# Layer 2 attention: probabilities of the later key blocks added onto the first block by POOL and DVE, one block summed by PE, values copied by ACT

## The reference, cut to what matters

```
xn = layernorm(x);  q = xn @ Wq.T;  k, v = split(xn @ Wkv.T)
q, k = 4 * l2norm(q), 4 * l2norm(k)
sim  = q @ k.T, masked above the diagonal
attn = softmax(sim);  out = layernorm((attn @ v) @ Wout.T) * g2
x = x + out + silu_gated_ffn(xn)
```

## Time and profile before

| | |
|---|---|
| median of three runs | 1303.96 us |
| the profiled execution's own time, and its span | 1300.34 us, 1298.5 us |
| busy over the span: PE, DVE, ACT, POOL | 1168.2, 892.5, 669.9, 466.3 us |
| weight loads (PEld) | 800.5 us |
| one body of layer 2 (974 to 1054 us) | 80.00 us, of which the rounds take 57.3 |
| DMA over the span | 23 GB/s mean |

### The profile page before, as it was taken

One profiled execution on the slowest core, in us unless ns is written; L12 is line 12 of the kernel. 1 busy time (PEld: TensorE's weight loads), 2 busy tenths in 40 slices (PEclk: granted clock), 3 DMA queues, 4 the chain that ended last, 5 costly groups with the idle time before them and its releaser, 6 DMA issues. The chain is left out here.

```text
span 1298.5 us, 27029 instructions
## 1 busy us (share of the span) xinstructions
PE 1168.2 (90%) x8812; PEld 800.5 (62%) x8812; DVE 892.5 (69%) x2474; ACT 669.9 (52%) x1294; POOL 466.3 (36%) x695
## 2 busy tenths in 40 slices
PE   4999999999999994798199899998999989999896
PEld 2656666565666643798165766657666675766665
DVE  6888888888888856465355766657666576665744
ACT  2667676766767661354064452644526355263540
POOL 4222212222221225553344362634525345263430
PEclk8999999999999995799699999999999999999998
DMA  2310001000100006123000000000000000000000
GB/s 67 100 24 17 18 18 25 17 17 20 23 17 18 23 4 210 45 63 55 8 10 1 9 8 0 16 0 8 8 0 16 0 10 6 0 16 0 9 1 9
DMA packets 34597, 29.78 MB, mean 23 GB/s; under 512 B 5984, under 2 KB 27104, under 8 KB 34528
## 3 DMA queue, kind: packets, MB, share of 16 engines
q1 hardware_dynamic: 32224, 24.22, 6.9%
q0 software_dynamic: 2304, 4.72, 1.7%
HBM read 13.72 MB, written 6.82 MB: 16 GB/s over the span
## 5 line engine op out<-in xcount | busy, mean ns | idle before, releaser
L1272 ACT ACTIVATE arena<-ring_a 128x384 f32<-128x384 f32 (+1 forms) x512 | 252.7, 550 | 138.6 <-PE ring_a L470 138.6
L1417 ACT ACTIVATE arena<-ring_a 128x1024 f32<-128x1024 f32 x128 | 131.6, 1028 | 160.1 <-PE ring_a L470 160.0
L1040 POOL TENSOR_SCALAR_AFFINE_SELECT arena<-arena 128x512 f32<-128x512 f32 x128 | 81.9, 640 | 356.9 <-ACT arena L1272 356.9
L470 PE MATMUL ring_a<-q_max,rows 128*128 128x384 f32 (+1 forms) x512 | 195.4, 385 | 0.9 <-ACT arena L1272 0.5
L1547 DVE CUSTOM_DVE_ANT_0 arena<-pair,arena 128x384 bf16<-128x384 f32 (+1 forms) x271 | 162.3, 614 | 26.4 <-PE pair L470 23.4
L1176 POOL TENSOR_TENSOR q_len<-q_sum,exponents 128x8 f32<-128x8 f32 x64 | 108.1, 1689 | 149.1 <-DVE q_sum L1836 149.1
L470 PE MATMUL pair<-arena,v_aug 128*64 128x512 f32 (+3 forms) x1024 | 150.2, 438 | 4.0 <-ACT arena L1417 3.5
L470 PE MATMUL ring_a<-rows,k_rows 64*128 64x384 f32 (+2 forms) x1152 | 124.8, 339 | 14.8 <-DVE rows L1854 13.8
L470 PE MATMUL ring_a<-arena,v_aug 128*32 128x384 f32 (+1 forms) x1024 | 122.8, 551 | 1.9 <-POOL arena L1040 1.0
L470 PEld LDWEIGHTS pair<-arena,v_aug 128*64 128x64 f32 x1024 | 68.3, 136 | 85.4 <-issue 69.2
L470 PE MATMUL pair<-rows,q_rows 128*128 128x384 f32 (+1 forms) x271 | 110.5, 410 | 3.2 <-DMA rows<-k_rows 2.6
(11 more groups left out here) (251 smaller groups left out, 2196.6 us busy)
## 6 DMA issues: line engine op xcount, KB each, us to landing
rows<-k_rows SPq DMA_DIRECT2D x128, 64.0 KB, 2.0
arena<-in_w SPq DMA_DIRECT2D x2, 2048.0 KB, 14.1
slots_y<-arena SPq DMA_DIRECT2D x40, 64.0 KB, 1.8
x_all<-in_x SPq DMA_DIRECT2D x8, 256.0 KB, 4.0
tokens_x<-xn_all SPq DMA_DIRECT2D x1, 2048.0 KB, 9.6
out<-o_t SPq DMA_DIRECT2D x8, 256.0 KB, 2.3
arena<-tokens_x,tokens_now POOLq DMA_INDIRECT x40, 2.8
wq_sb<-in_wq_t SPq DMA_DIRECT2D x1, 512.0 KB, 4.9
```

Source lines behind the costliest of these rows:

```text
L470: return pe.matmul(out, lhs, rhs, start=start, stop=stop, skip_group_check=True)
L1040: pool.affine_select(out=v, in_=v, compare_op=ALU.is_ge, fill=0.0, base=0, pattern=[[0, HG], [1 if late else -1, P]], channel_multiplier=- ...
L1272: act.activation(probs[:, t % NT, h, 0:many], A.slot(("cols", c))[:, 0:many], ACT.Exp).then_inc(A.free.sem, A.free.add(1))
L1417: act.activation(dst, src, ACT.Exp).then_inc(ring.free.sem, ring.free.add(1))
```

## The change

`sums1(0)` to `sums1(2)` take only block 0; before that, the probabilities of the later blocks have been added onto it. For this, `fold(n)` on POOL waits for `values1(n)`, adds block 3 onto block 2 (128 x 2 heads x 128) and block 2 onto block 1 (128 x 2 x 256); `fold(n)` on DVE adds block 1 onto block 0 (128 x 2 x 384). This is done for rounds 0 to 5; rounds 6 and 7 (`sums1(3)`) keep all blocks. The sums move from after rounds 2, 4 and 6 to after rounds 3, 5 and 7. POOL's `q_length` moves behind the masks of its round. `values_out` moves from DVE to ACT.

Sixteen matmuls leave the end of round 2, and four of them, the ones 512 columns wide, stand at the end of round 3. The diff's core:

```
@@ PE
+                    pe.wait_ge(s["folded"].sem, s["folded"].at(b, min(2 * m + 2, NP - 2)))
                     for j in range(NT):
                         for h in range(HG):
+                            n = 2 * m + h // 2
+                            if j == 0 or m == NP // 2 - 1:
+                                ins = mm(...)
...
                         values1(n - 1)
-                        if n % 2 == 0:
-                            sums1(n // 2 - 1)
+                        if n % 2 and n > 1:
+                            sums1((n - 3) // 2)
@@ POOL
+                def fold(n):
+                    pool.wait_ge(s["o_full"].sem, s["O"].filled(b, ("o", n)))
+                    apart(pool)
+                    third, fourth = (probs1[:, n % PB, 0:512].rearrange("p (c t) -> p c t", c=2),
+                                     probs1[:, n % PB, 512:1536].rearrange("p (c t) -> p c t", c=2)[:, :, 384:512])
+                    pool.tensor_tensor(third[:, :, 128:256], third[:, :, 128:256], fourth,
+                                       ALU.add).then_inc(s["folding"].sem, s["folding"].add(1))
+                    pool.wait_ge(s["folding"].sem, s["folding"].at(b, n + 1))
+                    second = probs1[:, n % PB, 512:1536].rearrange("p (c t) -> p c t", c=2)[:, :, 128:384]
+                    pool.tensor_tensor(second, second, third, ALU.add).then_inc(s["low_folded"].sem, s["low_folded"].add(1))
...
                 for n in range(NP):
-                    if n + 2 < NP:
-                        q_length(s, n + 1, b)
...  (the masks)
+                    if n + 2 < NP:
+                        q_length(s, n + 1, b)
+                    if 0 < n < NP - 1:
+                        fold(n - 1)
                     if not last and n == 0:
                         fetch_slots(b + 1)
@@ ACT
+                def values_out(n):
+                    ring = L if n == NP - 1 else O
+                    act.wait_ge(ring.full.sem, ring.filled(b, ("o", n)))
+                    act.activation(o1[:, n, :], ring.slot(("o", n))[:], ACT.Copy).then_inc(ring.free.sem, ring.free.add(1))
...  (at the end of round n)
+                    if n:
+                        values_out(n - 1)
+                values_out(NP - 1)
@@ DVE
+                def fold(n):
+                    dve.wait_ge(s["low_folded"].sem, s["low_folded"].at(b, n + 1))
+                    apart(dve)
+                    first, second = (probs1[:, n % PB, at:at + 1024].rearrange("p (c t) -> p c t", c=2) for at in (1536, 512))
+                    dve.tensor_tensor(first[:, :, P:T], first[:, :, P:T], second[:, :, 0:384],
+                                      ALU.add).then_inc(s["folded"].sem, s["folded"].add(1))
                 for n in range(NP):
+                    if n > 1:
+                        fold(n - 2)
                     if n + 2 < NP:
                         q_sums(s, n + 1, b)
...
-                    if n:
-                        values_out(n - 1)
...
-                values_out(NP - 1)
```

More of the change, by code:

```diff
@@ L96 @@
              e_full=10, e_free=9, own=18, var=1, veps=1, rstd=1,
-             sums=6, lens=6, q_lo=8, h1=3, masked=24, pv=4, g_free=2, inverted=1, fin=1, stored=16)
+             sums=6, lens=6, q_lo=8, h1=3, masked=24, low_folded=6, folding=6, folded=6, pv=4, g_free=2, inverted=1, fin=1, stored=16)
 CREDITED = dict(q_lo=1, q_free=1, o_free=1, l_free=1, s_free=1, m_free=1, w_free=1, e_free=1, g_free=1, sums=1, h1=1, r_free=1, added=1, stored=1, pv=1,
@@ L815, in sums1 @@
                         pe.wait_ge(s["g_free"].sem, s["g_free"].at(b, 0))
+                    pe.wait_ge(s["folded"].sem, s["folded"].at(b, min(2 * m + 2, NP - 2)))
                     for j in range(NT):
                         for h in range(HG):
-                            ins = mm(gather[32 * h:32 * h + 32, j * P:T], pick_sum[:, m, :], p_of(2 * m + h // 2, h % 2, j),
-                                     start=(m == 0 and j == 0), stop=(m == NP // 2 - 1 and j == NT - 1))
+                            n = 2 * m + h // 2
+                            if j == 0 or m == NP // 2 - 1:
+                                ins = mm(gather[32 * h:32 * h + 32, j * P:T], pick_sum[:, m, :], p_of(n, h % 2, j),
+                                         start=(m == 0 and j == 0), stop=(m == NP // 2 - 1 and j == NT - 1))
                     ins.then_inc(s["pv"].sem, s["pv"].add(1))
@@ L1185, in attend @@
                 s = SC
-                for name in ("veps", "rstd", "lens", "masked"):
+                for name in ("veps", "rstd", "lens", "masked", "low_folded", "folding"):
                     s[name].restart()
@@ L1332, in _ @@
             phase_end(act, 2)
-            credit(act, SC["s_free"], SC["m_free"], SC["w_free"])
+            credit(act, SC["s_free"], SC["m_free"], SC["w_free"], SC["o_free"], SC["l_free"])
             def move_x(b):
@@ L1378, in attend @@
                 s = SC
-                Q, S, M, W = (s[k] for k in "QSMW")
-                for name in ("s_free", "m_free", "w_free", "squared"):
+                Q, O, L, S, M, W = (s[k] for k in "QOLSMW")
+                for name in ("s_free", "m_free", "w_free", "o_free", "l_free", "squared"):
                     s[name].restart()
@@ L1786, in _ @@
             phase_end(dve, 2)
-            credit(dve, SC["q_free"], SC["o_free"], SC["l_free"], SC["e_free"], SC["g_free"], SC["sums"], SC["h1"], SC["q_lo"], SR["added"], SR["r_free"], SR["sums"])
+            credit(dve, SC["q_free"], SC["e_free"], SC["g_free"], SC["sums"], SC["h1"], SC["q_lo"], SR["added"], SR["r_free"], SR["sums"])
             def inverse(s, length, dst, k, b, scale):
@@ L1872, in attend @@
                 O, L, S, W, Z = (s[k] for k in "OLSWZ")
-                for name in ("q_free", "o_free", "l_free", "e_free", "own", "var", "sums", "q_lo", "h1", "g_free", "inverted", "fin"):
+                for name in ("q_free", "e_free", "own", "var", "sums", "q_lo", "h1", "g_free", "folded", "inverted", "fin"):
                     s[name].restart()
```

## The result

The changed kernel takes 1332.07 us (median of four runs, 1330.39 to 1332.32) against 1303.49 beside it: a ratio of 1.0209 with a 95% interval of 1.0195 to 1.0224, 28.6 us slower. The forecast was 1346, the range 1299 to 1380. The profiled execution has 1331.94 us, 31.6 over that of before; 4.3 of these lie in earlier phases, which the change does not touch (the first scores of layer 2 come at 658.2 us and not at 653.9).

A forecast was written before the change was run, and what follows sets the result against it. PE bounds the kernel before, POOL's in-order queue after. A body with a successor costs -1.0 + 6.0 + 1.2 = +6.2 us, seven +43, the last -1: +42, so 1346 us on the median; range 1299 to 1380.

The forecast's parts named there:

- The bound passes from PE to POOL's queue: Layer 2's rounds: POOL is late next, so PE waits for scaled queries and, at the body's end, the folded block.
- The sums: `sums1` on PE: 1.37 of 2.29 us goes from each of 24, 33 us if PE stays the bound.
- PE stays the bound: Rival: PE still sets the pace and the full 33 us go, 1271 us; chance 0.05.
- The chain on POOL: POOL, masks of round 2 to those of round 7: unhindered 32.9 us against 32.2 before, 0.7 more.
- the hindrance: POOL and DVE's two-operand SBUF operations delay each other: between 0 and 11.3 us a body, taken as 6.0.
- The small scaling: DVE's 8-column scaling stands behind POOL's first add, 0.6 us more; in rounds 4 and 5 together 1.2 a body.
- serial end: Rival of full exclusion between DVE and POOL: all 11.3 us serial, +11.5 a body, 1384 us; chance 0.12.
- The chain's start: POOL's masks of round 2 start at 992.5 against 994.24, 1.7 us less.
- The last body: Layer 2's final body, without fetches, experts or roots: at best PE's 4.1 us less, taken as -1.
- a body with a successor: Each of seven bodies of layer 2: -1.0 + 6.0 + 1.2 = +6.2 us, together +43.
- light hindrance: Rival: POOL and DVE hinder each other by only 3 us, +2.0 a body, 1317 us; chance 0.18.
- the unhindered queue: Rival of POOL's queue alone: the engines miss each other, a body 1.0 us shorter, 1293 us; chance 0.11.

The follow-up runs named there:

- e2: Changed kernel with all adds left out, sums short and at their new places: 1277.28 us, 0.9801 of the kernel before.
- e6: Changed kernel with POOL's `root` one round later, behind the masks of rounds 5 and 6: 1320.53 us, 1.0129 of the kernel before.
- e7: Changed kernel with all three adds on DVE at the head of its round, none on POOL: 1324.06 us, 1.016 of the kernel before.
- e1: Kernel before the change with only ACT copying the values and POOL's power behind the masks, no adds, sums whole: 1306.19 us, 1.0022.
- e12: Changed kernel with POOL's adds as fills and DVE's block add as a one-operand row sum: 1317.43 us, 1.0101 of the kernel before.
- e3: Changed kernel with POOL's two adds replaced by fills of the same duration that read nothing: 1324.78 us, 1.0162 of the kernel before.
- e4: Changed kernel with DVE's block add replaced by a row sum of one operand: 1323.38 us, 1.0151 of the kernel before.

## Why the prediction was right, and where it was off

*The bound passes from PE to POOL's queue: right.* PE's waits for scaled queries and the 37.5 us stretch say so, `e2` against the change shows that the adds do it, and `e6` that the order of POOL's queue has a part in it. How much of the 55 us is POOL's adds and how much DVE's is not shown: `e7`, with none on POOL and three on DVE, is slow as well.

*The sums: 1.37 us each, 33 in all.* Measured 1.29 (2.29 to 1.00), and `e2` 28.9 under `e1`: right; 24 x 1.29 is 31, and where the other 2 went is not shown. The rival that PE stays the bound (1271) is what `e2` shows without adds.

*Costs of the operations: right.* DVE's add 0.97 (taken 1.0), POOL's 0.73 and 1.33 (0.74 and 1.29), ACT's copies 0.60 and nearly free (`e1`).

*The chain on POOL: right in kind, 37.5 where the sum gave 40.1* (32.9 + 6.0 + 1.2). The term that was too large is the hindrance. Over the stretch the masks of rounds 2 to 6 are 2.25 us above 1.49 each, the powers 0.46 above 1.64 each and the two `veps` 1.0 above 0.23 each: 3.7 us and not 6.0 (`rstd` of round 5, 1.33, was as long before). The power, which the prediction had as no reading, was held too: 2.02 us where it starts behind a `q_low` of DVE, at 1031.51. The small scaling costs 2 x 0.54 in rounds 4 and 5, near the 1.2 taken. What is left, 32.7, is near the 32.9 without hindrance. Single operations did hold each other as in the 1.66 us row, but of the 11.3 us that could have met, POOL lost a third: that two operations which meet exclude each other did not put the sum toward its serial end, as the prediction had it.

*The chain's start: -1.7 expected, -1.0 measured* (19.05 against 20.09 us from the body's first scores to the masks of round 2). The second add of round 1 was hindered (1.61 for 1.27), while my sum counted hindrance from round 2 on only, and the hand-offs ahead of the adds and of the fetches took 0.2 each; the two fetches took the 2.6 taken.

*The last body: -1 expected, -2.7 measured*, from the last two reciprocals, after and then before (76.2 us apart against 78.9, by the unrounded starts):

```profile
L1946 DVE RECIPROCAL m_cols<-gather x2: 3357/3357/3357, 1228.9 to 1305.0; 128x512 f32<-128x512 f32 x2
```

```profile
L1919 DVE RECIPROCAL m_cols<-gather x2: 3357/3357/3357, 1194.7 to 1273.6; 128x512 f32<-128x512 f32 x2
```

So a body with a successor costs 4.3 instead of 6.2 (the six distances between the earlier reciprocals have a mean of 84.3 against 80.0); seven are 30, less 2.7 is 27, which is what the profiled execution has in layer 2 (31.6 less 4.3). The result lies between the forecast of 1346 and the light hindrance of 1317, the body's 4.3 half-way between 6.2 and 2.0. The range from 1299 to 1380 holds both, so that it was met does not tell them apart.

*What the runs put in another light.* I had the unhindered queue as a gain (1293) and the hindrance as the whole loss. With the adds' collisions away, `e12` is still at +13. It is not free of hindrance: masks, `q_low` and the small scaling still meet. By my own terms 6.3 of the 11.3 us of DVE's two-operand work are left, POOL reads SBUF for the masks alone (7.5 of 32.9 us, 0.23 of the time), and the 1.2 stays: 1293 + 7 x 2.6 = 1311 against 1317. In its trace the masks of rounds 2 to 6 are 2.1 us above 1.49 each, nearly as in the change, the powers 0.4 above 1.64, and the small scaling still costs 2 x 0.5. So `e12` agrees with the sum better than with the word: a queue in which nothing waits passes every delay on, whichever operation has it. That `e3` and `e4` gained only half of what was expected fits: others took their place. With POOL's adds no longer held, the masks of rounds 2 and 3 met DVE (2.03 us each in `e3`, 1.69 and 1.71 in the change); in `e4` it was the power of round 3 (2.11 for 1.68) and the masks of round 5 (1.95 for 1.61). An unhindered POOL was not tried, since the masks themselves read SBUF; how much of `e12`'s +13 is queue and how much is their collisions stays open.

## What to carry to other kernels

Work that is taken off the bounding engine pays where the receiving engine has a pause at the point in its order at which the work becomes ready. Here an engine that was half-idle in the mean had no such point, and an in-order queue without pauses passed every collision and every wait at its head on to the rest. Look for the place by what the engine waits for and by what waits for the result, and check both ends: here the same two adds on DVE gave 1306.8, 1309.4 and 1300.2 us in three places. Before adding up the gains of edits that remove collisions one by one, expect that others take their place.

## What the runs showed of the hardware

POOL's fill, which reads nothing, neither held DVE's two-operand operations nor was held by them: all 48 long fills of `e3` took 1271 to 1284 ns, and a second operation of `silu_up` that ran wholly beside one (from 1007.38, the fill from 1007.16) took its usual 0.69 us. But a fill held the one-operand scaling of 8 columns, 0.157 us alone, for up to 0.695 (1010.90 in `e12`, 0.07 behind a fill). The Trainium skill ("SBUF — State Buffer", section "Who interferes with whom") has both cases apart, two operands against POOL's reads and the two-port mode of a scaling against any access. These rows agree in what is held and what is not; in which mode the scaling ran, no row shows.
